# z convolved in its own row, statistics and shifts moved off VectorE, y copied sooner: a three-stage state-space kernel

## What is computed

```python
x = x + 0.5 * ffn(layernorm(x))      # routed mixture: 16 experts, 4 picked, and 2 shared ones
x = x + attn(layernorm(x))           # the state-space block
x = x + 0.5 * ffn(layernorm(x))      # the same weights again
```

```python
xz = jnp.transpose(hidden_states @ W_in, (0, 2, 1))
x, z = jnp.split(xz, 2, axis=1)
x = jax.nn.gelu(_dwconv_same(x, K_x, b_x), approximate=False)     # u in the kernel
z = jax.nn.gelu(_dwconv_same(z, K_z, b_z), approximate=False)
x_dbl = jnp.einsum('bdl,de->ble', x, W_xproj)
dt, Bm, Cm = jnp.split(x_dbl, [DT_RANK, DT_RANK + D_STATE], axis=-1)
delta = jax.nn.softplus(dt + b_dt[None, :, None])
y = _selective_scan(x, delta, A, Bm, Cm, D)       # h = exp(delta*A)*h + delta*B*u; y = sum(C*h) + D*u
y = jnp.transpose(jnp.concatenate([y, z], axis=1), (0, 2, 1))
return y @ W_out
```

## Time and profile before

| what | value |
|---|---|
| median of 3 runs | 912.05 us (912.02 to 912.63) |
| the profiled execution, its own time | 912.01 us |
| its span | 910.2 us |
| PE busy | 868.7 us, 95% of the span |
| DVE busy | 729.9 us, 80% |
| POOL busy | 650.8 us, 71% |
| ACT busy | 540.2 us, 59% |
| granted TensorE clock, mean | 0.994 of full |

### The profile page before, as it was taken

How to read it: one execution, slowest core, us unless ns; L and a number is a source line. 1 busy time by engine, 2 the same in 40 slices (tenths; PEclk the granted TensorE clock), 3 DMA queues, 4 the chain that set the end, 5 groups by cost and what they waited for, 6 DMA issues and landing times. The chain is left out here.

```text
span 910.2 us, 12224 instructions
## 1 busy us (share of the span) xinstructions
PE 868.7 (95%) x3591; PEld 621.9 (68%) x3591; DVE 729.9 (80%) x1257; ACT 540.2 (59%) x951; POOL 650.8 (71%) x476
## 2 busy tenths in 40 slices
PE   8999999999999998999999977799999999999997
PEld 7777778877767775455445433477787788788885
DVE  4989878877975567999999989978896787696664
ACT  7565565565554668767776574246556556555554
POOL 7758776766756567898898877846576677676765
PEclk9999999999999999999999998999999999999999
DMA  8715374353343342444344443251627545545450
GB/s 205 222 53 157 125 203 122 113 152 128 94 138 108 91 122 97 151 142 154 133 151 161 131 144 120 80 159 47 182 76 197 157 132 150 158 112 162 152 128 23
DMA packets 120611, 121.33 MB, mean 133 GB/s; under 512 B 55001, under 2 KB 78689, under 8 KB 120545
## 3 DMA queue, kind: packets, MB, share of 16 engines
q1 hardware_dynamic: 102352, 116.35, 42.4%
q10 hardware_dynamic: 18192, 4.21, 2.1%
HBM read 111.87 MB, written 8.65 MB: 132 GB/s over the span
## 5 line engine op out<-in xcount | busy, mean ns | idle before, releaser
L714 POOL TENSOR_TENSOR act_lo<-act,act_hi 128x512 fp32r<-128x512 f32 x288 | 372.3, 1297 | 208.5 <-ACT act_hi L827 208.3
L820 ACT ACTIVATE bank<-bank 128x512 f32<-128x512 f32 x252 | 146.6, 582 | 239.3 <-PE bank L1155 220.3
L1051 DVE TENSOR_TENSOR sg<-bank,c_ring 128x512 f32<-128x512 f32 x252 | 172.2, 683 | 95.0 <-ACT bank L820 88.2
L1151 PE MATMUL bank<-x_parts,w_hi 128*128 128x512 f32 x572 | 234.4, 410 | 10.2 <-DVE act L1029 7.5
L1029 DVE SCALAR_TENSOR_TENSOR act<-sg,bank 128x512 f32<-128x512 f32 x288 | 197.8, 687 | 38.6 <-PE bank L1155 20.7
L1155 PE MATMUL bank<-x_parts,w_hi 128*128 128x512 f32 x572 | 225.8, 395 | 0.0
L1152 PE MATMUL bank<-x_parts,w_lo 128*128 128x512 f32 x572 | 225.6, 394 | 0.0
L827 ACT ACTIVATE act_hi<-act 128x512 fp32r<-128x512 f32 x288 | 179.3, 623 | 1.0 <-PE bank L1127 0.8
L1151 PEld LDWEIGHTS bank<-x_parts,w_hi 128*128 128x128 f32 x572 | 107.6, 188 | 48.3 <-DVE act L1029 16.5
L1152 PEld LDWEIGHTS bank<-x_parts,w_lo 128*128 128x128 f32 x572 | 107.7, 188 | 25.5 <-issue 2.6
L1155 PEld LDWEIGHTS bank<-x_parts,w_hi 128*128 128x128 f32 x572 | 107.6, 188 | 25.5
(11 more groups left out here) (177 smaller groups left out, 992.3 us busy)
## 6 DMA issues: line engine op xcount, KB each, us to landing
c_ring<-c_dram SPq DMA_DIRECT2D x252, 256.0 KB, 3.8
c_ring<-c_dram SPq DMA_DIRECT2D x64, 512.0 KB, 3.6
y_dram<-out_t SPq DMA_DIRECT2D x56, 64.0 KB, 2.9
y_tok<-y_dram SPq DMA_DIRECT2D x14, 256.0 KB, 3.7
xt_dram<-xn ACTq DMA_DIRECT2D x32, 64.0 KB, 3.6
xt<-xt_dram ACTq DMA_DIRECT2D x8, 256.0 KB, 3.3
out<-x_sb SPq DMA_DIRECT2D x7, 256.0 KB, 2.3
x_sb<-in_L_attn_hidden_states SPq DMA_DIRECT2D x3, 512.0 KB, 6.1
```

What stands on the lines that cost most here:

```text
L714: self.nc.gpsimd.tensor_tensor(m["act_lo"][:, g % LAG], m["act"][:, g % ACTS], m["act_hi"][:, g % LAG].bitcast(FP32), ALU.subtract).then_i ...
L820: nc.scalar.activation(self.s_bank[:, g % 2], self.h_bank[:, g % 2], ACT.Silu).then_inc(self.sg_ready, 1)
L1051: nc.vector.tensor_tensor(m["sg"][:, g % 2], silu, weight, ALU.mult).then_inc(self.w_done, 1)
L1151: nc.tensor.matmul(dst, m["w_hi"][:, k, n, :], x_hi, start=True, stop=False)
```

## The change

**z is made later.** The convolution of z is taken out of the first mixture, and in steps of row i TensorE convolves z of row i itself instead of row i + 2, for rows 0 to 5. z of rows 6 and 7 follows in row 6, in steps n = 1 to 4, where no convolution stood; z of row 6 goes into the bank half that took x, z of row 7 into the half that takes the projection, whose step for row 5 moves from n = 4 to n = 6 of row 6. ScalarE takes both of these gelus after its step 53 (`LAST_Z`), with a load of the gelu tables ahead and of the exponential's behind. `x_pad` gets three rows, z one buffer in place of three. VectorE's routing of row 0, which uses a bank that z of row 6 passes through, waits for these gelus. ScalarE's copy of the projected row 5 moves to step 56.

**The head is closed up.** With z gone, the lists put the gelu of u after block 121 (125 before), B and C's copies after 125 (128) and delta's softplus after 128 (131).

**Statistics and shifts.** The statistics of row 6 for the state-space stage move from VectorE's step 24 into the first mixture, after block 140; those of row 7 from step 25 to step 24. The two shifts that VectorE made in steps 27 and 45 become two GpSimd instructions each, right behind the root (`pool_shift`): times -1, then times the root.

**y sooner.** In step n = 3 ScalarE copies y first and makes the decays after.

Cut to its core:

```diff
-HEAD_DVE = (101, 102, 104, 106, 107, 109, 110, 120, 121, 134)
-HEAD_POOL = (102, 107, 120, 129)
-HEAD_ACT = (105, 106, 109, 113, 117, 120, 124, 125, 128, 131, 135, 137)
-HEAD_PE = (108, 111, 112, 115, 116, 119, 122, 123, 127, 130, 133, 134)
-FRONT_DVE = {41: 1, 43: 1, 45: 1, 54: 2, 55: 2, 56: 2, 57: 2, 58: 1, 59: 1, 60: 1, 61: 1, 62: 1}
+HEAD_DVE = (101, 102, 104, 106, 107, 109, 110, 120, 121, 134, 140)
+HEAD_POOL = (102, 107, 120, 126)
+HEAD_ACT = (105, 106, 109, 113, 116, 120, 121, 125, 128, 137)
+HEAD_PE = (108, 111, 112, 115, 118, 119, 124, 127)
+FRONT_DVE = {41: 1, 43: 1, 54: 2, 55: 2, 56: 2, 57: 2, 58: 1, 59: 1, 60: 1, 61: 1, 62: 1}
...
+    def pool_shift(self, pool, r, rows):
+        nc, m = self.nc, self.m
+        q = slice(r % NORMS, r % NORMS + rows)
+        pool.wait_ge(self.rstd_ready, r + rows)
+        nc.gpsimd.tensor_scalar(m["var_eps"][:, q, :], m["mean_var"][:, q, :, 0], -1.0, None, ALU.mult
+                                ).then_inc(self.mean_turned, rows)
+        pool.wait_ge(self.mean_turned, r - BATCH - 6 + rows)
+        nc.gpsimd.tensor_tensor(m["shift"][:, q, :], m["var_eps"][:, q, :], m["rstd"][:, q, :], ALU.mult
+                                ).then_inc(self.shift_ready, rows)
...
     def pool_front_pieces(self, pool):
         self.norm.pool_root(pool, self.first, 2)
+        self.norm.pool_shift(pool, self.first, 2)
...
         dve.wait_ge(self.score_ready, b + 1)
+        if self.mamba and r == 0:
+            dve.wait_ge(self.mamba.z_gated, BATCH)
...
-        norm.dve_shift(dve, self.first, 2)
-        yield
         yield from self.dve_route(dve, 0, 1)
...
                 if n == 2 and i == 3:
                     self.norm.pool_root(pool, BATCH + 6, 2)
+                    self.norm.pool_shift(pool, BATCH + 6, 2)
...
+    def act_gelu_z(self, ae, i):
+        ae.wait_ge(self.conv_z, i + 1)
+        if i < BATCH - 2:
+            need(ae, self.out_ready, i)
+        self.nc.scalar.activation(self.z_row(i), self.z_bank(i), ACT.Gelu, bias=self.m["b_z_sb"][:, 0:1]
+                                  ).then_inc(self.z_gated, 1)
...
+        return self.front[:, 1] if i < BATCH - 2 else self.front[:, 0] if i == BATCH - 2 else self.misc
...
+                if n == 3 and i:
+                    self.act_y(ae, i - 1)
                 if g + 2 < ALL_PAIRS:
                     self.act_decays(ae, g + 2)
...
-                if n == 3 and i:
-                    self.act_y(ae, i - 1)
...
-                if n == 6 and i:
+                if n == 6 and i and i != BATCH - 2:
                     self.act_x(ae, i - 1)
+                if g == ALL_PAIRS - PAIRS:
+                    self.act_x(ae, i - 2)
...
-                    self.act_gelus(ae, i + 2)
+                    self.act_gelu_u(ae, i + 2)
+                    self.act_gelu_z(ae, i)
                     self.nc.scalar.preload_act_table_set("softplus")
+                if g == LAST_Z:
+                    self.act_gelu_z(ae, BATCH - 2)
+                    self.act_gelu_z(ae, BATCH - 1)
+                    self.nc.scalar.preload_act_table_set("exp_and_others")
...
+        dve.wait_ge(self.f1.x_added, BATCH - 1)
+        norm.dve_stats(dve, 2 * BATCH - 2)
+        norm.dve_aggregate(dve, 2 * BATCH - 2)
+        yield
...
-                if i == 3:
-                    if n in (0, 1):
-                        dve.wait_ge(self.f1.x_added, i + 4 + n)
-                        norm.dve_stats(dve, BATCH + i + 3 + n)
-                        norm.dve_aggregate(dve, BATCH + i + 3 + n)
-                    if n == 3:
-                        norm.dve_shift(dve, BATCH + i + 3, 2)
+                if i == 3 and n == 0:
+                    dve.wait_ge(self.f1.x_added, BATCH)
+                    norm.dve_stats(dve, 2 * BATCH - 1)
+                    norm.dve_aggregate(dve, 2 * BATCH - 1)
...
+                if i < BATCH - 2:
                     if n == 3:
                         pe.wait_ge(self.delta_ready, i + 2)
-                        self.pe_conv(pe, i + 2, 1, [0], front[:, 1, :])
+                        self.pe_conv(pe, i, 1, [0], self.z_bank(i))
...
+                if i == BATCH - 2:
+                    if n == 1:
+                        pe.wait_ge(self.rows_copied, 2 * BATCH)
+                        self.pe_conv(pe, i, 1, [0, 1], self.z_bank(i))
+                    if n == 2:
+                        self.pe_conv(pe, i, 1, [2, 3], self.z_bank(i))
+                    if n == 3:
+                        pe.wait_ge(self.x_added, i - 1)
+                        self.pe_conv(pe, i + 1, 1, [0, 1], self.z_bank(i + 1))
+                    if n == 4:
+                        self.pe_conv(pe, i + 1, 1, [2, 3], self.z_bank(i + 1))
+                if n == (6 if i == BATCH - 2 else 4) and i:
+                    if i == BATCH - 2:
+                        pe.wait_ge(self.z_gated, BATCH)
                     need(pe, self.xt_copied, min(i + 3, BATCH))
                     self.pe_project_out(pe, i - 1, range(TT))
```

More of the change, by code:

```diff
@@ L33 @@
 RING = 4
+LAST_Z = (BATCH - 2) * PAIRS + 5
 ADDED = 1, 5, 6
@@ L99, in program @@
         act_hi = sb("act_hi", [P, LAG, SEQ], F32R)
-        with nc.sbuf_tensor("z_third", [P, SEQ], FP32) as z_third:
-            pass
         act_lo = sb("act_lo", [P, LAG, SEQ], F32R)
@@ L374, in pool_first @@
         assert steps.n == self.SELECTS
-        for v in (m["x_pad"][:, 0:1], m["x_pad"][:, SEQ + 1:SEQ + TAPS - 1], m["bc_parts"][:].bitcast(FP32)):
+        for v in (m["x_pad"][:, :, 0:1], m["x_pad"][:, :, SEQ + 1:SEQ + TAPS - 1], m["bc_parts"][:].bitcast(FP32)):
             nc.gpsimd.memset(v, 0.0).then_inc(self.edges, 1)
@@ L710, in pool_blocks @@
                 g = i * NE + k
-                if self.mamba and g == 0:
-                    pool.wait_ge(self.mamba.out_ready, BATCH - 2)
                 pool.wait_ge(self.hi_ready, g + 1)
@@ L1252, in __init__ @@
         self.staged = room[:, RING * size:(RING + 2) * size].rearrange("p (a s l) -> p a s l", a=2, s=2)
-        assert (RING + 2) * size <= NE * 3 * P
+        self.z = room[:, (RING + 2) * size + P:(RING + 2) * size + P + SEQ]
+        assert (RING + 2) * size + P + SEQ <= NE * 3 * P
         self.bc_rows = m["bc_rows"]
-        self.z_rows = m["z"][:, 0], m["z"][:, 1], m["z_third"][:, :]
         def sem(name):
@@ L1347, in act_copy_xt @@
         ae.wait_ge(self.norm.xt_ready, BATCH + r + 1)
-        need(ae, self.conv_z, r)
-        self.nc.scalar.activation(self.m["x_pad"][:, 1:SEQ + 1], src, ACT.Copy).then_inc(self.xt_copied, 1)
-    def act_raw(self, ae, r, h, src):
-        ae.wait_ge(self.conv_z if h else self.conv_x, r + 1)
-        dst = self.z_rows[r] if h else self.m["u"][:, r]
-        self.nc.scalar.activation(dst, src, ACT.Copy).then_inc(self.raw_copied, 1)
+        need(ae, self.conv_z, r - 2)
+        self.nc.scalar.activation(self.m["x_pad"][:, r % 3, 1:SEQ + 1], src, ACT.Copy).then_inc(self.xt_copied, 1)
@@ L1357, in act_gelu_first_u, with act_raw, act_gelu_u @@
+    def act_raw(self, ae, r, src):
+        ae.wait_ge(self.conv_x, r + 1)
+        self.nc.scalar.activation(self.m["u"][:, r], src, ACT.Copy).then_inc(self.raw_copied, 1)
     def act_gelu_first_u(self, ae):
         m = self.m
-        ae.wait_ge(self.raw_copied, 3)
+        ae.wait_ge(self.raw_copied, 2)
         self.nc.scalar.activation(m["u"][:, 0:2], m["u"][:, 0:2], ACT.Gelu, bias=m["b_x_sb"][:, 0:1]).then_inc(self.u_gated, 2)
         self.nc.scalar.preload_act_table_set("silu_and_others")
-    def act_gelus(self, ae, r):
-        nc, m = self.nc, self.m
+    def act_gelu_u(self, ae, r):
+        m = self.m
@@ L1365, in act_gelus @@
         ae.wait_ge(self.conv_x, r + 1)
[L1366 to L1374 removed]
+        self.nc.scalar.activation(m["u"][:, r % 3], self.front[:, 0, :], ACT.Gelu, bias=m["b_x_sb"][:, 0:1]
+                                  ).then_inc(self.u_gated, 1)
@@ new lines, in act_gelu_z, with z_row @@
+    def act_gelu_z(self, ae, i):
[4 more added lines that the diff above has]
+                                  ).then_inc(self.z_gated, 1)
+    def z_row(self, i):
+        if i < BATCH - 2:
+            return self.z
+        return self.m["u"][:, (BATCH - 3) % 3] if i == BATCH - 2 else self.m["x_pad"][:, (BATCH - 3) % 3, 0:SEQ]
@@ L1429, in act_head @@
         yield
-        self.act_raw(ae, 0, 0, misc)
-        yield
-        self.act_raw(ae, 0, 1, misc)
+        self.act_raw(ae, 0, misc)
         yield
@@ L1435, in act_head @@
         yield
-        self.act_raw(ae, 1, 0, misc)
+        self.act_raw(ae, 1, misc)
         yield
@@ L1577, in pe_conv @@
         for k in taps:
-            last = nc.tensor.matmul(dst, m["w_tap"][:, h, k, :], m["x_pad"][:, k:k + SEQ],
-                                    start=(k == 0), stop=(k == TAPS - 1))
+            last = nc.tensor.matmul(dst, m["w_tap"][:, h, k, :], m["x_pad"][:, r % 3, k:k + SEQ],
+                                    start=(k == 0), stop=(k == TAPS - 1), skip_group_check=True)
         if TAPS - 1 in taps:
```

(12 more changed lines are left out.)

33 lines of the change are left out of this document (11 added, 22 removed).

## The result

The changed kernel takes 906.31 us (median; 905.8 to 907.63) beside 912.03 us of the kernel before on the same chip: ratio 0.9943, 95% interval 0.9928 to 0.9958, so 5.7 us are won (4 to 7). The forecast was 900.8 us, and its range ended at 905.0: the gain came out at half of what I expected.

What follows compares the result with a forecast made beforehand. TensorE was taken to bound the first mixture and VectorE the state-space stage, with TensorE nearly as full. The sum was 912.0 - 5.8 - 1.0 - 2.3 - 2.8 + 0.75 = 900.8 us, range 898.6 to 905.

Steps and rivals of the forecast that it cites:

- Term 1: First mixture: z's convolutions leave TensorE, 6.9 us off, 1.1 us back through ScalarE's delays: -5.8 us.
- give-back: First mixture: TensorE standing after gelu 0.9 and softplus 0.4 us, less 0.2 of before: 1.1 us come back.
- z's matmuls were not on the path: Rival, first mixture: TensorE would stand as long for VectorE, so removing z's matmuls gains nothing: 906.6 us, chance 0.06.
- the rival on the clock: Rival, row 6: TensorE's clock falls to 1.2 GHz while the new matmuls run and stays there: 924 us, chance 0.03.
- Term 2: State-space stage: row 6's statistics move to the first mixture, inside VectorE's slack behind block 140: -1.0 us.
- Term 3: State-space stage: two shifts leave VectorE for GpSimd, saving 0.2 us at the first, 2.1 at the second: -2.3 us.
- Term 4: Row 6: y copied 1.2 us sooner, TensorE keeps its clock, VectorE's standing goes: -2.8 us, bounds -1.2 and -2.84.
- Term 5: Row 6: z of rows 6 and 7 made there costs 0.25 us at step 53, 0.5 at step 54: +0.75 us.

Runs made afterwards that it cites:

- e1: The changed kernel with VectorE's third shift of the head after block 124 in place of 121: 900.72 us, ratio 0.9869 to the kernel before.
- e8: The changed kernel with VectorE's third head shift, the gelu and the pieces behind it, and row 7's logits all placed later: 899.78 us, ratio 0.9871.
- e2: The changed kernel with the gelu after block 125 (was 121) and its partner pieces after 127 to 131: 904.18 us, ratio 0.9921.
- e7: The kernel before with only VectorE's third shift of the head moved, after block 124 in place of 121: 911.45 us, ratio 0.9995.
- e11: The changed kernel with VectorE's third head shift after block 124 and the moved statistics back at their places of before: 901.17 us, ratio 0.9887.
- e10: The kernel before with only the two shifts of the state-space stage moved to GpSimd: 909.24 us, ratio 0.9970.
- e5: The changed kernel with the two shifts of the state-space stage back on VectorE: 911.87 us, ratio 1.0001 to the kernel before.
- e9: The kernel before with only the copy of y put ahead of the decays in every row: 909.93 us, ratio 0.9983.
- e4: The changed kernel with the copy of y behind the decays again in all rows: 908.59 us, ratio 0.9958 to the kernel before.

## Why the prediction was wrong, and where it was right

**Term 1 failed, in its give-back.** That z's 6.9 us of matmuls were on the path was right: e1 and e8 reach the first scan at 346.10 and 346.37 us, against 346 forecast. The step that failed is the one that let 1.1 us come back. It took the delay of ScalarE by the gelu piece against TensorE's slack of 1.94 us, measured at block 143, where VectorE has nothing in its queue but the block's own products. At block 121 VectorE's queue holds the third shift, tied through GpSimd's root to ScalarE's rounding. The profile before had the 2.43 us wait of that shift, and the new lists had the three pieces within two blocks of each other. I read the lists for ScalarE and TensorE, and not for GpSimd and VectorE. In place of 0.9 us TensorE stood 5.33 us, about 2.8 of them by the gelu's place and 2.5 by the wait of the next paragraph, and lost some 2 us more at half clock, for which the term had nothing. Where nothing meets, the prediction's way of reckoning is on the safe side: 0.30 us for the gelu and 0.27 for softplus in e1, against 0.9 and 0.4.

**A second omission in the same term**: two of z's four pairs were the work that hid the shift's 2.43 us, and I never asked what the removed work covered (e2 against e7: 2.5 us).

The rival "z's matmuls were not on the path" gave 906.6 us, near the result of 906.31, for a reason that the runs refute: that nearness is chance. It had 0.06. A rival with a new wait in the first mixture was missing altogether; the rival on the clock looked for it in row 6.

**Term 2**: forecast 1.0, stage 1.02 (e11). **Term 3**: forecast 2.3, alone 2.2 in the stage and 2.7 by the median (e10); undone in the changed kernel it was worth 3.7 in the stage (e5), since the first shift can be caught too. **Term 4**: forecast 2.8, alone 2.5 in the stage (e9). Its mechanism, standing plus clock, is shown; its bounds of 1.2 and 2.84 are the two measured cases, e4 and nearly e9. **Term 5**: forecast 0.25 at step 53 and 0.5 at step 54; the changed kernel has 0.20 and 0.42 more there than before, and VectorE stands 0.59 us once. Before, step 53 to 54 had a wait for ScalarE of its own, 0.26 us, which went.

The prediction cites the Trainium skill on table sets (ScalarE: Activation LUTs, Rules for kernel authors): by its 2.7 us for each switch term 1 would have been near 0. The term did come out near 0 (first scan at 352.09 us in place of 351.85), but not for that. The loads took 1.28 us each, and the whole piece 3.76 us, as before.

## What to carry to other kernels

When work is placed by lists, one for each engine, follow a moved piece through every queue, not only its own: what stands behind it on its engine, who waits for that in which other queue, and what stands there. Before work is taken off the engine that sets the pace, look for waits of the other engines beside it that it covers; they come to light when it goes. And a short instruction is priced by what it may have to wait for, not by its shortest row.
